# First attention of a fused two-layer network: the order of the first tiles on five engines

## The reference, cut to what matters

```python
x = x + l0_xattn(layernorm(x), ctx, Wq, bq, Wk, bk, fn_w, qn_w, kn_w)

def l0_xattn(text, features, ...):
    fn = rmsnorm(features, fn_w)
    Q = rmsnorm(text @ Wq + bq, qn_w)
    K = rmsnorm(fn @ Wk + bk, kn_w)
    scores = Q @ K.T / sqrt(512)        # within each batch of 64 rows
    return softmax(scores) @ fn
```

## Time and profile before

| | |
|---|---|
| median of 3 runs | 1511.59 us |
| the profiled execution's own time | 1511.27 us |
| its span in the profile | 1509.5 us |
| mean granted TensorE clock | 0.994 |
| TensorE busy | 1463.2 us (97%) |
| VectorE busy | 1127.8 us (75%) |
| ScalarE busy | 795.1 us (53%) |
| GpSimd busy | 710.3 us (47%) |

### The profile page before, as it was taken

How to read it: one execution, slowest core, us unless ns; L and a number is a source line. 1 busy time by engine, 2 the same in 40 slices (tenths; PEclk the granted TensorE clock), 3 DMA queues, 4 the chain that set the end, 5 groups by cost and what they waited for, 6 DMA issues and landing times.

```text
span 1509.5 us, 27579 instructions
## 1 busy us (share of the span) xinstructions
PE 1463.2 (97%) x9895; PEld 846.4 (56%) x9895; DVE 1127.8 (75%) x2172; ACT 795.1 (53%) x3201; POOL 710.3 (47%) x668
## 2 busy tenths in 40 slices
PE   5999999999999799999999999999999999999998
PEld 4888745555555455555555555555565555555554
DVE  5788787878876888776776676677677677667868
ACT  5678841211223576556546654754664565565763
POOL 5668875454565353334334343433434333343553
PEclk9999999999999999999999999999999999999999
DMA  7454435333344565653553554455445445334622
GB/s 248 147 175 136 123 81 126 98 77 50 65 88 72 117 147 84 110 119 64 100 105 53 95 88 81 86 87 95 81 80 105 79 73 103 64 60 67 99 50 112
DMA packets 358936, 146.87 MB, mean 97 GB/s; under 512 B 342304, under 2 KB 342688, under 8 KB 356112
## 3 DMA queue, kind: packets, MB, share of 16 engines
q1 hardware_dynamic: 357504, 137.77, 45.1%
q10 hardware_dynamic: 1296, 7.34, 1.5%
HBM read 58.02 MB, written 4.19 MB: 41 GB/s over the span
## 4 chain that ended last, share of the span: by engine, by line
PE 55%; DVE 5%; ACT 3%; DMA 1%; POOL 1%; issue 1%; SPq 0%; DVEq 0%; POOLq 0%; ACTq 0%
PE bank L72 18%; PE bank L74 17%; PE bank L73 17%; PE bank L2439 3%; ACT a_prob L1836 2%; DMA a_pT_lo<-a_p_lo 1%; POOL a_prob L1707 1%; DVE a_oT_lo L2106 1%; DVE x_res L2193 1%; DVE a_qve L2045 1%; ACT a_oT_lo L1813 0%; DVE a_p_lo L2094 0%; DVE a_nmx L2082 0%; DVE a_qr_lo L2035 0%; POOL a_xr_lo L1731 0%
## 5 line engine op out<-in xcount | busy, mean ns | idle before, releaser
L1836 ACT ACTIVATE a_prob<-a_prob,a_nmx 128x64 f32<-128x64 f32 x512 | 170.2, 334 | 183.7 <-DVE a_nmx L2082 183.7
L72 PE MATMUL bank<-w,a_oT_hi 128*128 128x512 f16 x512 | 194.0, 379 | 1.8 <-DVE a_oT_lo L2106 0.9
L74 PE MATMUL bank<-w,a_oT_hi 128*128 128x512 f16 x512 | 194.0, 379 | 0.0
L73 PE MATMUL bank<-w,a_oT_lo 128*128 128x512 f16 x512 | 194.0, 379 | 0.0
L72 PE MATMUL bank<-w,xT_hi 128*128 128x448 f16 (+1 forms) x512 | 188.0, 367 | 3.1 <-DVE h L1231 2.0
L73 PE MATMUL bank<-w,xT_lo 128*128 128x448 f16 (+1 forms) x512 | 187.7, 367 | 0.0
L74 PE MATMUL bank<-w,xT_hi 128*128 128x448 f16 (+1 forms) x512 | 187.5, 366 | 0.0
L1707 POOL TENSOR_TENSOR a_prob<-a_prob,a_mask 128x512 f32<-128x512 f32 x64 | 79.8, 1268 | 204.5 <-DVE a_prob L2076 204.5
L2031 DVE SCALAR_TENSOR_TENSOR x_res<-bank,a_oinv,x_res 128x512 f32<-128x512 f32 x128 | 95.5, 746 | 75.0 <-PE bank L74 75.0
L1157 ACT CAST f_h_hi<-h 128x448 f16<-128x448 f32 x64 | 35.6, 563 | 209.7 <-DVE h L1231 209.6
L1719 POOL TENSOR_TENSOR a_krs<-a_kve,neg_half 128x4 f32<-128x4 f32 x32 | 32.8, 1026 | 239.6 <-DVE a_kve L2056 239.6
(11 more groups left out here) (351 smaller groups left out, 4120.5 us busy)
## 6 DMA issues: line engine op xcount, KB each, us to landing
shared<-in_l_wq SPq DMA_DIRECT2D x8, 1024.0 KB, 5.0
shared<-in_l_wo SPq DMA_DIRECT2D x8, 1024.0 KB, 5.1
shared<-in_w ACTq DMA_DIRECT2D x8, 896.0 KB, 4.7
craw<-in_w SPq DMA_DIRECT2D x11, 512.0 KB, 3.9
a_wide<-in_l_ctxT SPq DMA_DIRECT2D x16, 256.0 KB, 4.0
x_res<-in_x SPq DMA_DIRECT2D x16, 256.0 KB, 4.5
shared<-in_ctx SPq DMA_DIRECT2D x16, 256.0 KB, 4.4
shared<-in_l_wkv SPq DMA_DIRECT2D x8, 512.0 KB, 3.9
```

The source lines that it names most:

```text
L72: pe.matmul(out, a_hi, b_hi, start=first, stop=False)
L73: pe.matmul(out, a_lo, b_hi, start=False, stop=False)
L74: return pe.matmul(out, a_hi, b_lo, start=False, stop=last)
L1836: ins = act.activation(pt, pt, ACT.Exp, bias=nmx[:, col:col + 1], accum_out=den[:, col:col + 1])
```

## The change

- SP: the bias `bq` is loaded before `fnw`, and both count on one semaphore. The transposed context of tile 2 no longer waits for the squares and weighed features of tile 0; only the context of tile 2 does.
- GpSimd: tile 1's row root stands ahead of its features root. In `body(0)` the key root of tile 1 stands ahead of `tile_roots(0)`, and `weigh(1)` moves from the opening to behind `features_T(2)`.
- ScalarE: in the opening the copy of tile 0's queries stands ahead of `normalise(1)`, and `rows_T(1)` ahead of `query_squares(0)`. `body(0)` has a list of its own, `first_body`. The first two loads of w1 move from the opening to the end of `first_body`.
- VectorE: `wqk` is made before `rows_T(0)`; `query_bias(0)` stands ahead of `scale_keys(0)`; `statistics(2)` stands between the low parts of tile 0's queries and keys, and `statistics(3)` moves into `body(0)`, which has a list of its own.
- TensorE: `project_k(1)` is cut in three, with `q_T(0)` after its first 6 matmuls and `k_T(0)` after 3 more. In `body(0)` the keys are turned before the queries.

No instruction is added or taken away. The diff, cut to its core (the new functions `q_T`, `k_T`, `exps`, `scores`, `denominators` and `probs_T` hold the lines that stood in `qk_T` and `body`):

```diff
@@ -318,18 +318,22 @@
         load_cT(1)
         sp.dma_start(qnw[:, :], a.l0_qnw.partition_broadcast(P)).then_inc(const_in, 16)
         sp.dma_start(wqk, a.l0_knw.partition_broadcast(P)).then_inc(const_in, 16)
-        sp.dma_start(fnw, a.l0_fnw.partition_broadcast(P)).then_inc(fnw_in, 16)
-        sp.dma_start(bq, a.l0_bq.partition_broadcast(P)).then_inc(const_in, 16)
+        sp.dma_start(bq, a.l0_bq.partition_broadcast(P)).then_inc(bq_fnw_in, 16)
+        sp.dma_start(fnw, a.l0_fnw.partition_broadcast(P)).then_inc(bq_fnw_in, 16)
         load_x(1)
         load_c(1)
         load_x(2)
         sp.wait_ge(wl_ok, 2 * KD)
         load_x(3)
         for n in range(2, NT):
-            sp.wait_ge(s_css, n - 1)
-            sp.wait_ge(s_cw, n - 1)
+            if n > 2:
+                sp.wait_ge(s_css, n - 1)
+                sp.wait_ge(s_cw, n - 1)
             sp.wait_ge(s_cTl, n - 1)
             load_cT(n)
+            if n == 2:
+                sp.wait_ge(s_css, 1)
+                sp.wait_ge(s_cw, 1)
             load_c(n)
             if n + 2 < NT:
...
@@ -361,7 +365,7 @@
             if n:
                 pool.wait_ge(s_fl, n)
             else:
-                pool.wait_ge(fnw_in, 16)
+                pool.wait_ge(bq_fnw_in, 32)
             pool.tensor_tensor(cw[:, :], craw[:, bass.ts(n % 2, D)], fnw, ALU.mult).then_inc(s_cw, 1)
...
@@ -413,11 +417,16 @@
             root(krs[:, :], kss[:, :], 1.0, L0_EPS, s_krs)
 
         def body(n, first=False, ahead=True, project=True):
+            if first:
+                key_root(1)
             tile_roots(n)
             if ahead:
                 features_T(n + 2)
+            if first:
+                weigh(1)
             if project:
-                key_root(n + 1)
+                if not first:
+                    key_root(n + 1)
                 pool.wait_ge(s_kn, n + 2)
...
@@ -448,12 +457,11 @@
         first_features_root(0)
         features_T(1)
         key_root(0)
+        first_row_root(1)
         first_features_root(1)
-        first_row_root(1)
         weigh(0)
         first_row_root(2)
         features_lo(0)
-        weigh(1)
         pool.wait_ge(s_eps, 1)
...
@@ -479,9 +487,9 @@
             act.wait_ge(c_in_, (n + 1) * 16)
             if n >= 3:
                 act.wait_ge(s_root, n - 2)
-            if n == 1:
-                act.wait_ge(s_kss, 1)
-            elif n >= 2:
+            if n in (1, 2):
+                act.wait_ge(s_kss, n)
+            elif n >= 3:
                 act.wait_ge(s_qss, n - 1)
             act.activation(sq, craw[:, bass.ts(n % 2, D)], ACT.Square, scale=MEAN, accum_out=css(n)).then_inc(s_css, 1)
...
-            act.wait_ge(s_css, min(n + 2, NT) if n else 1)
+            act.wait_ge(s_css, min(n + 2, NT) if n >= 2 else n + 1)
...
         def load_w1(n, p):
-            if n < 6:
+            if 0 < n < 6:
                 act.wait_ge(s_wmx, n - 1)
-            else:
+            elif n >= 6:
                 act.wait_ge(w1l_ok, 2 * p - 2)
             act.dma_start(w1_raw[p % 2], a.w1[:, p * W1P:(p + 1) * W1P]).then_inc(w1_in[p % 2], 16)
...
+        def first_body():
+            normalise(2)
+            key_squares(1)
+            squares_c(2)
+            features_T(2)
+            rows_T(2)
+            k_T(1)
+            exps(0)
+            q_T(1)
+            probs_T(0)
+            query_squares(1)
+            features(1)
+            load_w1(0, 0)
+            load_w1(0, 1)
+
         def body(n, first=False, ahead=True, project=True):
+            if first:
+                first_body()
+                return
...
-                qk_T(n + 1)
-            act.wait_ge(s_pT, n + 1)
-            wait_features_root(act, n)
-            act.activation(pT_hi[:, :], b_pT, ACT.Copy, scale=crs(n)).then_inc(s_pTh, 1)
+                q_T(n + 1)
+                k_T(n + 1)
+            probs_T(n)
...
@@ -612,14 +647,13 @@
         rows_T(0)
         split_wq((2, 3))
         features_T(1)
-        for n in range(2):
-            act.dma_start(w1_raw[n], a.w1[:, n * W1P:(n + 1) * W1P]).then_inc(w1_in[n], 16)
         key_squares(0)
         squares_c(1)
+        q_T(0)
         normalise(1)
-        qk_T(0)
+        k_T(0)
+        rows_T(1)
         query_squares(0)
-        rows_T(1)
         features(0)
         run(body)(act)
...
+        def first_body():
+            key_bias(1)
+            statistics(3)
+            scale_keys(1)
+            dve.wait_ge(s_qss, 1)
+            query_bias(1)
+            scores(0)
+            rows_T(2)
+            denominators(0)
+            k_T(1)
+            q_T(1).then_inc(s_kTl, 1)
+            probs_T(0)
+            statistics(4)
+
         def body(n, first=False, ahead=True, project=True):
+            if first:
+                first_body()
+                return
...
@@ -782,21 +844,22 @@
         statistics(0)
         split_wk((2, 3))
         split_wq((0, 1))
+        dve.wait_ge(const_in, 32)
+        dve.scalar_tensor_tensor(wqk, qnw[:, :], float(D) ** -0.5, wqk, ALU.mult, ALU.mult).then_inc(wqk_ok, 1)
         rows_T(0)
         split_wq((2, 3))
         dve.wait_ge(bk_in, 16)
         key_bias(0)
-        dve.wait_ge(const_in, 48)
         statistics(1)
-        dve.scalar_tensor_tensor(wqk, qnw[:, :], float(D) ** -0.5, wqk, ALU.mult, ALU.mult).then_inc(wqk_ok, 1)
+        dve.wait_ge(bq_fnw_in, 32)
+        query_bias(0)
         dve.wait_ge(wqk_ok, 1)
         dve.wait_ge(off_ok, 2)
         scale_keys(0)
-        query_bias(0)
-        qk_T(0)
+        q_T(0)
+        statistics(2)
+        k_T(0).then_inc(s_kTl, 1)
         rows_T(1)
-        statistics(2)
-        statistics(3)
...
-        def project_k(n, first=False):
-            pe.wait_ge(s_cTl, n + 1)
-            for k in range(KD):
+        def project_k(n, first=False, ks=range(KD)):
+            if 0 in ks:
+                pe.wait_ge(s_cTl, n + 1)
+            for k in ks:
                 if first:
                     pe.wait_ge(wl_ok, k + 1)
                 ins = split_mm(pe, bk_bank[:, :], cT_hi[:, k, :], cT_lo[:, k, :], w_hi[1][:, k, :], w_lo[1][:, k, :],
                                k == 0, k == KD - 1)
-            ins.then_inc(s_k, 1)
+            if KD - 1 in ks:
+                ins.then_inc(s_k, 1)
...
-            if project:
+            if first:
+                k_T(1)
+                q_T(1)
+            elif project:
                 q_T(n + 1)
                 k_T(n + 1)
...
@@ -898,9 +966,11 @@
         rows_T(0)
         project_q(0, first=True)
         pe.wait_ge(s_kb, 1)
-        project_k(1)
+        project_k(1, ks=range(0, 2))
         q_T(0)
+        project_k(1, ks=range(2, 3))
         k_T(0)
+        project_k(1, ks=range(3, KD))
         rows_T(1)
```

More of the change, by code:

```diff
@@ L236, in l0_attention @@
     xT_lo, cT_lo, qT_lo, kT_lo = (xT4_lo[:, :, n * P:(n + 1) * P] for n in range(4))
-    const_in, bk_in, fnw_in, fnwT_in = sem("const_in"), sem("bk_in"), sem("fnw_in"), sem("fnwT_in")
+    const_in, bk_in, bq_fnw_in, fnwT_in = sem("const_in"), sem("bk_in"), sem("bq_fnw_in"), sem("fnwT_in")
     wq_in, wk_in = ([sem(f"{w}{k}_in") for k in range(2)] for w in ("wq", "wk"))
@@ L527, in query_squares, with q_T, k_T @@
             act.activation(sq, qb[:, :], ACT.Square, scale=MEAN, accum_out=qss).then_inc(s_qss, 1)
-        def qk_T(n):
+        def q_T(n):
             act.wait_ge(s_qT, n + 1)
             act.copy(qT_hi[:, :, :], blk(bqT)).then_inc(s_qTh, 1)
+        def k_T(n):
             act.wait_ge(s_kT, n + 1)
@@ L555, in first_rows, with probs_T, exps @@
                            scale=m.ln_rs[:, t:t + 1]).then_inc(prep.norm if t == TPC - 1 else s_n0, 1)
+        def probs_T(n):
+            act.wait_ge(s_pT, n + 1)
+            wait_features_root(act, n)
+            act.activation(pT_hi[:, :], b_pT, ACT.Copy, scale=crs(n)).then_inc(s_pTh, 1)
+        def exps(n):
+            act.wait_ge(s_nmx, n * 2 + 2)
+            act.activation(prob[:, :], prob[:, :], ACT.Exp, bias=nmx[:, :], accum_out=den[:, :]).then_inc(s_p, 1)
+        def first_body():
[12 more added lines that the diff above has]
+            load_w1(0, 1)
         def body(n, first=False, ahead=True, project=True):
+            if first:
+                first_body()
+                return
             if ahead:
@@ L568, in body @@
                 before_exps()
-            act.wait_ge(s_nmx, n * 2 + 2)
-            act.activation(prob[:, :], prob[:, :], ACT.Exp, bias=nmx[:, :], accum_out=den[:, :]).then_inc(s_p, 1)
+            exps(n)
             if ahead:
@@ L652, in scale_keys, with q_T, k_T @@
             dve.scalar_tensor_tensor(kn[:, :], kb[:, :], krs[:, :], wqk, ALU.mult, ALU.mult).then_inc(s_kn, 1)
-        def qk_T(n):
+        def q_T(n):
             dve.wait_ge(s_qTh, n + 1)
-            dve.tensor_tensor(qT_lo[:, :, :], blk(bqT), qT_hi[:, :, :], ALU.subtract)
+            return dve.tensor_tensor(qT_lo[:, :, :], blk(bqT), qT_hi[:, :, :], ALU.subtract)
+        def k_T(n):
```

(29 more changed lines are left out.)

## The result

The change made the kernel slower: 1514.1 us median over 20 runs (1511.32 to 1516.37) against 1511.1 (20 runs, 1507.85 to 1514.86), a ratio of 1.0021 with a 95% interval of 1.0014 to 1.0027. That is 3.0 us, about the 0.2% that can be told from no change. The forecast was 1505.8 us and its range ended at 1509.4.

The account below looks back on a forecast made before the run. TensorE, busy 97% of the span, was taken as the bound, with 6.45 us idle and 2.41 us of half clock before 48.25. `project_k(3)` at 42.8 instead of 48.25 gave 1511.27 - 5.45 = 1505.8 us; range 1503.0 to 1509.4.

Parts of the forecast that it names:

- The chain up to `project_k(2)`: Opening and body 0: earlier scores, loads and roots let `project_k(2)` start at 30.9 us, not 36.90; 6.0 of 6.45 idle.
- The place of the next wait: Tile 3's loads are late next; ScalarE's squares or VectorE's statistics wait, with a 2 to 3 us gap before `project_k(3)`.
- the chain from the context's landing to `project_k(3)`: Tile 1's squares, `normalise(3)`, copies, key squares, key root, scale and turn: together 5.8 us from landing to `project_k(3)`.
- the landing of tile 3's context beside w1: Context issued at 32.5 takes 4.5 us beside w1, lands at 37.0; `project_k(3)` starts at 42.8.
- The 6.3 of the earlier trace: An x load's time beside w1, taken as the nearest row; it would give landing 38.8 and `project_k(3)` at 44.6.
- Rival B: Tile 3's loads starve beside w1: context lands at 40.1, `project_k(3)` at 45.9, 2.35 us gained, 1508.9; chance 0.13.
- D: Slower: tile 3's context moves only after w1, lands 43.0; `project_k(3)` at 48.8, half clock returns, +3.0 us, 1514.2; chance 0.03.
- The second step: VectorE's opening: early `wqk` costs 0.66 wherever it stands; if knw is late `rows_T(0)` waits, bounds 0 and 0.66, taken 0.
- The third: TensorE's clock before 48.25 us: keeping the 2.4 GHz level gains 2.41 us, bounds 0 and 2.41.
- Rival C: Clock falls anyway, between 28.3 and 30.9 or 38 and 42.8: 2.41 us comes back, 3.0 gained, 1508.2; chance 0.17.

## Why the prediction was wrong

*What held.* The chain up to `project_k(2)` was right in its order and nearly in its sizes. Scores of tile 0 were put at 24.1 and came at 25.42, the end of the roots at 29.5 and 30.83, `project_k(2)` at 30.9 and 32.27: every stage 1.3 to 1.4 us late, and the lag is already there at `q_T(0)` (20.73 forecast, 22.03 measured). One end time on the way doesn't follow from its row: `weigh(0)` was put at 23.9, where its own row gives 23.01 + 1.27 = 24.28; it ended at 24.21. It cost nothing, since ScalarE came to those squares only at 28.06, without a wait. The place of the next wait was right too: ScalarE's squares and VectorE's statistics, both for tile 3's round of loads. And the chain from the context's landing to `project_k(3)` was put at 5.8 us (its terms add up to 5.7); it was 5.9 (42.35 to 48.26) in one profile and 6.3 in the other.

*The step that failed* is the landing of tile 3's context beside w1. I took 4.5 us, "near the middle" of 2.9 and 6.3, "because this load starts with w1, not in the thick of it". It took 8.6 and 8.3 in the two profiles. The miss at `project_k(3)`, 5.46 us, is this one in the main: 1.27 for the round issued at 33.77 and not 32.5, 4.1 for the load, 0.1 for the chain behind it. Two things in that sentence were wrong. The 6.3 of the earlier trace rows was no upper bound: that x tile was issued 3 us after w1, with only the rest of w1 in its way, whereas here all of it was. And starting together was the worse place, not a mild one: 8.0 to 8.6 in all four profiles in which context and w1, in its large packets, start together on two queues. Undoing the collision in three ways (w1 in the opening, w1 in the idle stretch, small packets) each brought the time to about 2 us under before, some 4 to 5 under the changed kernel, with intervals clear of its own; that is shown. The rule cited from *DMA: Bandwidth & Descriptors* of the Trainium skill (Queues, rings and completion order), turns between queues packet by packet, should have carried the sum. The trace agrees with it: 266 and 308 packets in the same 6 us with 1.71 and 0.58 MB, and 765 and 838 once w1's packets were small. Rival B was this mechanism, priced at a landing of 40.1 and 45.9 for `project_k(3)`. B had the round at 32.2 and the load at 7.9; they came at 33.77 and took 8.6, so the context landed at 42.35, with w1's second piece, and gave 48.26: close to D's figure, without D's cause, since the context moved beside w1 and not behind it.

*The second step* is `wqk`, put at 0 with an upper bound of its own duration, 0.66. The bound left out the wait in front of it. Where the product waited for it, knw landed at 13.9 to 15.7; the copy that `rows_T(0)` needs is there at 13.5 to 16.1, later where x tile 0 comes later. In the profile I worked from x had come late (copy at 15.70) and knw landed at 15.0, so the product would just have fitted in. Every kernel with `wqk` early waited longer before `project_q(0)` than the 1.40 of before, by 0.3 to 1.6 us. In the first profile of the changed kernel the wait only used up what the sooner x tile had given; its 1.3 us lag is that of the half clock in `project_q(0)`, which the sum put at nothing and which falls there in profiles with `wqk` late too. What making `wqk` early costs in time isn't settled: taking it back won 0.17% with w1 in the idle stretch, about 1 us (within the intervals) in the changed kernel, and nothing measurable with w1 in the opening or the other way round in the kernel before.

*The third* is the half clock, counted as a gain of 2.41 us. The second profile of before had it where it cost little, and ended 3.0 us sooner. The gain was that of one execution. In the changed kernel the stop of 4.58 us brought a new half clock, 0.89 and 0.78 over the stretch. Rival C named this, but as the only fault, not as a companion of B. It is also the likeliest source of the 3.0 us by which the change lost. The mean granted clock, which every run has, is 0.992 in the 31 runs of the changed kernel and 0.994 in 88 of the kernel before on three chips, and 0.995 to 0.996 in the six kernels whose traces show no wait of TensorE over 1.5 us from `project_k(2)` to 60 us. The first difference, 0.0017 before rounding, is at most 2.6 us of full speed over 1510 (an estimate). Where in those runs the clock fell only the profiles tell: behind the stop in all three that have the stop for tile 3. (In `project_q(0)` it fell in eight of the fourteen profiles, with and without that stop.)

In chances: B, C and D were given 0.33 together as if each came alone. They share one cause, a long stop of TensorE for tile 3, and so come together. The range ended where B alone ended.

## What to carry to other kernels

When an edit makes a chain some us shorter, list the loads that are triggered from inside it and ask what else starts on the DMA engines at that moment, above all transfers released by the same signal: here `weigh(1)` released tile 3's loads and w1 alike. Price a load beside another queue by the packets of the other that must pass while it moves; here a large transfer in large packets did best in an idle stretch, or behind the urgent loads in their own queue, in pieces, though the load just ahead of it (5.0 and 7.9 us) and the next round behind it (8.0 and 5.9) still paid. An instruction that is moved takes its wait along, so its bound is the wait's, read in more than one execution.

## What was not expected of the hardware

- Cutting one transfer into pieces with smaller packets made a *different* queue's load land 3.6 us sooner (8.6 to 5.0 us) and took 4.5 to 5.3 us off the kernel, while the next round's context took 9.0.
- A 1.8 MB transfer put on the same queue left the context load ahead of it at 3.0 us, but the x tile between them took 5.0 and the context of the next round 8.0.
- Two profiles of one and the same kernel differ by 2.5 us at `project_k(3)` before (45.7 against 48.25) and by 3.5 us at `project_k(4)` after (57.20 against 60.74). In the first pair it is the half clock of TensorE in another place, in the second that and a first x tile that came 1.5 us later.
